# An audio tower whose four engines' instruction sequences are written out in another order

## The reference, cut to what matters

```python
h = gelu(x @ W1 + b1); h = gelu(h @ W2 + b2)            # 750 x 512, exact gelu
lens = sigmoid(h @ W3 + b3); lens = lens / sum(lens) * 375
cs = cumsum(lens); P = max(cs[:, None] - arange(375), 0)
h = warp_weights(P) @ x                                 # 375 x 128
a = layernorm(h); q, k, v = split(rmsnorm(a) @ w_qkv)   # k and v get 8 memory columns
out = rmsnorm((softmax(k) @ v.T  applied to softmax(q)) @ w_out + b_out); h = h + out
xf = layernorm(h); expert = argmax(xf @ switch.T); p = max(softmax(xf @ switch.T))
pos = place of the token among all tokens of its expert so far
h = h + where(pos < capacity, xf @ W[expert].T + b[expert], xf) * p
```

## Time and profile before

| What | us |
|---|---|
| Runs, median (lowest to highest of three) | 393.8 (393.59 to 2108.33) |
| Profiled execution: span from first to last instruction | 392.4 |
| Median less that span | 1.4 |
| PE busy in it | 374.4 |
| DVE busy | 335.1 |
| ACT busy | 227.2 |
| POOL busy | 111.8 |

### The profile page before, as it was taken

One profiled execution on the slowest core, in us unless ns is written; L12 is line 12 of the kernel. 1 busy time (PEld: TensorE's weight loads), 2 busy tenths in 40 slices (PEclk: granted clock), 3 DMA queues, 4 the chain that ended last, 5 costly groups with the idle time before them and its releaser, 6 DMA issues. The chain is left out here.

```text
span 392.4 us, 7891 instructions
## 1 busy us (share of the span) xinstructions
PE 374.4 (95%) x2702; PEld 327.1 (83%) x2702; DVE 335.1 (85%) x916; ACT 227.2 (58%) x433; POOL 111.8 (28%) x136
## 2 busy tenths in 40 slices
PE   8999899999999999999999999999999989999892
PEld 8887788888889888888988888888887788998892
DVE  4687869969897999799988999899998975888896
ACT  4653369627971699159933994389537743782200
POOL 6121301031152216221522141403330501107880
PEclk9999999999999999999999999999999999999998
DMA  7768002002000110002000200100000070331134
GB/s 222 193 197 272 2 1 85 3 0 82 5 20 3 27 62 22 3 0 85 14 10 1 86 7 15 47 0 3 22 0 0 22 195 7 89 118 33 41 80 126
DMA packets 16406, 21.58 MB, mean 55 GB/s; under 512 B 4930, under 2 KB 11928, under 8 KB 15934
## 3 DMA queue, kind: packets, MB, share of 16 engines
q1 hardware_dynamic: 12398, 18.30, 16.1%
q0 software_dynamic: 2880, 2.35, 2.4%
q10 hardware_dynamic: 1088, 0.42, 0.4%
HBM read 14.40 MB, written 6.62 MB: 54 GB/s over the span
## 5 line engine op out<-in xcount | busy, mean ns | idle before, releaser
L1093 PE MATMUL psB<-W2h,h1l 128*125 128x512 f32 x184 | 74.6, 406 | 0.0
L1094 PE MATMUL psB<-W2l,h1h 128*125 128x512 f32 x184 | 72.5, 394 | 0.0
L1095 PE MATMUL psB<-W2h,h1h 128*125 128x512 f32 x184 | 72.5, 394 | 0.0
L668 ACT ACTIVATE h2b<-h2b 125x512 f32<-125x512 f32 x48 | 30.0, 628 | 30.9 <-DVE h2b L1640 30.5
L1095 PEld LDWEIGHTS psB<-W2h,h1h 128*125 128x125 f32 x184 | 34.1, 185 | 8.5
L1094 PEld LDWEIGHTS psB<-W2l,h1h 128*125 128x125 f32 x184 | 34.2, 186 | 6.9
L1093 PEld LDWEIGHTS psB<-W2h,h1l 128*125 128x125 f32 x184 | 34.2, 186 | 6.9
L1640 DVE TENSOR_TENSOR h2b<-psB,b2r 125x512 f32<-125x512 f32 x48 | 32.8, 685 | 4.5 <-PE psB L1095 4.4
L651 ACT ACTIVATE h<-psA,b1c 128x376 f32<-128x376 f32 x60 | 33.3, 579 | 5.7 <-PE psA L1040 3.9
L1647 DVE CUSTOM_DVE_ANT_0 h2b<-h2b,W3r 125x512 f32<-125x512 f32 x48 | 32.9, 690 | 1.6 <-ACT h2b L668 1.4
L531 POOL TENSOR_TENSOR dx<-xt 125x640 f32<-125x640 f32 x8 | 12.9, 1617 | 64.6 <-PE psC L1118 53.0
(11 more groups left out here) (284 smaller groups left out, 970.0 us busy)
## 6 DMA issues: line engine op xcount, KB each, us to landing
xTf<-in_x_t SPq DMA_DIRECT2D x16, 187.5 KB, 2.5
xt<-in_x SPq DMA_DIRECT2D x8, 336.0 KB
slot_x<-eb_parts SPq DMA_DIRECT2D x2, 960.0 KB, 11.9
basef<-in_L_tok_W SPq DMA_DIRECT2D x4, 256.0 KB, 5.3
ewT<-in_expert_t SPq DMA_DIRECT2D x1, 1024.0 KB, 8.0
ewf<-slot_x SPq DMA_DIRECT2D x2, 480.0 KB, 6.2
h2b<-slot_x SPq DMA_DIRECT2D x2, 480.0 KB, 8.2
slot_y<-h SPq DMA_DIRECT2D x4, 240.0 KB, 2.4
```

The lines of the kernel that those rows point to most:

```text
L668: nc.scalar.activation(slot, slot, ACT.Gelu).then_inc(c_g2.sem, 1)
L1093: mm(ps, lo, W2h[:, k, :], start=k == 0, stop=False)
L1094: mm(ps, hi, W2l[:, k, :], start=False, stop=False)
L1095: last = mm(ps, hi, W2h[:, k, :], start=False, stop=k == HK - 1)
```

## The change

`pipeline`, `step`, `opening` and `ending` are gone from TensorE, VectorE, ScalarE and GpSimd, and every call stands in a list, row by row, in another sequence. The calls are the same ones with the same arguments; functions, buffers, waits inside the functions, and SyncE's list stay. ScalarE's `setup` is now called inside `memory_keys` and TensorE's inside `sums`, for row 0 alone. The sequence differs in the opening, in each of the middle rows (which no longer follow one pattern) and in the ending. On ScalarE the exponentials and the gelus of a row stand in fewer separate runs: its list holds 30 table loads before and 19 now. `root_table`, a dummy square root, moves from the middle of the tail to its end.

```diff
 # GpSimd
-            def step(m, f, k, r):
-                if f is not None:
-                    sigmoid_pow(f, before(f))
-                if r is not None:
-                    scatter(r, before(r))
-                if m is not None:
-                    differences(m, before(m))
-                if f is not None:
-                    norm1(f, before(f))
...
-            def opening():
-                differences(0, None)
-                sigmoid_pow(0, None)
-                differences(1, 0)
-                norm1(0, None)
...
+            differences(0, None)
+            sigmoid_pow(0, None)
+            norm1(0, None)
+            differences(1, 0)
+            sigmoid_pow(1, 0)
...
+            counts(0, None)
+            scatter(0, None)
+            differences(2, 1)
+            sigmoid_pow(2, 1)
...
+            counts(3, 2)
+            scatter(3, 2)
+            differences(5, 4)
+            sigmoid_pow(5, 4)
...
+            fetch(3, 0, 3)
+            fetch(4, 0, 3)
+            fetch(0, 0, 3)
+            fetch(1, 0, 1)
+            fetch(1, 1, 3)
+            fetch(2, 0, 3)
+            fetch(5, 0, 3)
 # ScalarE
-                gelu2(LAST, 4)
-                memory_keys(PRIOR, 3)
-                gelu2(LAST, 5)
...
+            memory_keys(6, 1)
+            memory_keys(6, 2)
+            memory_keys(6, 3)
+            route_exp(5, 4)
+            key_exp(6, 5, 0)
+            key_exp(6, 5, 1)
+            key_exp(6, 5, 2)
+            gelu2(7, 2)
+            gelu2(7, 3)
+            gelu2(7, 4)
+            gelu2(7, 5)
 # TensorE
-                expert_products(6)
-                expert_products(7)
-                values(LAST, PRIOR, 1)
-                k_transposed(LAST, PRIOR, 0)
-                k_transposed(LAST, PRIOR, 1)
-                positions(PRIOR, None)
-                k_transposed(LAST, PRIOR, 2)
-                values(LAST, PRIOR, 2)
...
+            values(7, 6, 1)
+            values(7, 6, 2)
+            positions(6, None)
+            expert_products(5)
+            expert_tokens(7)
+            k_transposed(7, 6, 0)
+            k_transposed(7, 6, 1)
+            k_transposed(7, 6, 2)
+            expert_products(6)
+            expert_products(7)
+            chosen_on_rows(6)
+            context(7, 6)
 # VectorE
-                take_outputs(5)
-                query_sum(LAST, PRIOR)
-                take_outputs(7)
-                key_sum(LAST, PRIOR)
-                query_norm(LAST, PRIOR)
-                place_in_expert(PRIOR, PRIOR - 1)
...
+            place_in_expert(6, 5)
+            take_outputs(5)
+            query_sum(7, 6)
+            key_sum(7, 6)
+            query_norm(7, 6)
+            take_outputs(7)
+            own_experts(6)
```

More of the change, by code:

```diff
@@ new lines, in _ @@
+            bias2(1, 0, 5)
+            query_norm(0, None)
+            dot3(1, 0, 4)
+            dot3(1, 0, 5)
+            minus_z(1, 0)
+            scan(1, 0)
+            h1_lower(2, 1, 0)
+            lengths(1, 0)
+            warp_weights(1, 0)
+            bias2(2, 1, 0)
+            take_m(0, None)
+            x_lo_next(2)
+            dot3(2, 1, 0)
+            h1_lower(2, 1, 1)
+            moments1(1, 0)
+            normal1(1, 0)
+            out_norm(0, None)
+            residual(0, None)
@@ new lines, in _ @@
+            place_in_expert(0, None)
+            bias2(2, 1, 4)
+            dot3(2, 1, 3)
+            bias2(2, 1, 5)
+            query_sum(1, 0)
+            key_sum(1, 0)
+            dot3(2, 1, 4)
+            dot3(2, 1, 5)
+            minus_z(2, 1)
+            query_norm(1, 0)
+            scan(2, 1)
+            h1_lower(3, 2, 0)
+            lengths(2, 1)
+            warp_weights(2, 1)
+            bias2(3, 2, 0)
+            probability(0, None)
+            keep_base(0, None)
+            dot3(3, 2, 0)
@@ new lines, in _ @@
+            dot3(4, 3, 3)
+            bias2(4, 3, 5)
+            dot3(4, 3, 4)
+            dot3(4, 3, 5)
+            minus_z(4, 3)
+            query_norm(3, 2)
+            scan(4, 3)
+            h1_lower(5, 4, 0)
+            key_sum(3, 2)
+            probability(2, 1)
+            lengths(4, 3)
+            warp_weights(4, 3)
+            take_m(3, 2)
+            bias2(5, 4, 0)
+            keep_base(2, 1)
+            h1_lower(5, 4, 1)
+            moments1(4, 3)
+            normal1(4, 3)
@@ new lines, in _ @@
+            key_max(4, 3, 2)
+            key_max(4, 3, 3)
+            dot3(5, 4, 1)
+            dot3(5, 4, 2)
+            place_in_expert(3, 2)
+            probability(3, 2)
+            dot3(5, 4, 3)
+            bias2(5, 4, 4)
+            bias2(5, 4, 5)
+            query_sum(4, 3)
+            dot3(5, 4, 4)
+            key_sum(4, 3)
+            dot3(5, 4, 5)
+            minus_z(5, 4)
+            query_norm(4, 3)
+            scan(5, 4)
+            h1_lower(6, 5, 0)
+            lengths(5, 4)
@@ new lines, in _ @@
+            dot3(6, 5, 5)
+            minus_z(6, 5)
+            query_sum(5, 4)
+            scan(6, 5)
+            query_norm(5, 4)
+            lengths(6, 5)
+            warp_weights(6, 5)
+            h1_lower(7, 6, 0)
+            take_m(5, 4)
+            lower_biases()
+            moments1(6, 5)
+            keep_base(4, 3)
+            normal1(6, 5)
+            out_norm(5, 4)
+            residual(5, 4)
+            xn_lo(6, 5)
+            moments2(5, 4)
+            bias2(7, 6, 0)
@@ new lines, in _ @@
+            query_sum(6, 5)
+            dot3(7, 6, 2)
+            dot3(7, 6, 3)
+            keep_h(6, 5)
+            bias2(7, 6, 4)
+            bias2(7, 6, 5)
+            dot3(7, 6, 4)
+            dot3(7, 6, 5)
+            key_max(6, 5, 3)
+            scan(7, 6)
+            query_norm(6, 5)
+            lengths(7, 6)
+            warp_weights(7, 6)
+            keep_base(5, 4)
+            key_sum(6, 5)
+            take_m(6, 5)
+            moments1(7, 6)
+            normal1(7, 6)
+            out_norm(6, 5)
```

1766 lines of the change are left out of this document (1020 added, 746 removed).

## The result

The change made the kernel slower: 409.37 us median (408.98 to 410.1) against 394.22 of the kernel before, a ratio of 1.0393 with a 95% interval of 1.0377 to 1.041. Forecast were 390.5 us and a range of 386 to 395. The profiled execution has a span of 407.3 us, 14.9 more than before.

A forecast was written before the change was run, and what follows sets the result against it. TensorE was taken to bound the kernel up to take_outputs(7), then VectorE with the fetches beside it. -1.0 + 0 + 0.7 - 3.0 = -3.3 on 392.4 gave 389.1, with 1.4 for the median 390.5 us; range 386 to 395.

The forecast's parts named there:

- The middle rows: Five rows of 41 us up to row 7's first layer: no change, at most 1.2 us to gain, new waits up to 3.6.
- Its rule: Rival in two middle rows: scatter and differences delay sigmoid_pow in GpSimd's queue, 1.8 us a row, 3.6 in all; chance 0.12.
- The worst form: GpSimd queue rival at the old distance: sigmoid_pow 4.1 us late in two rows, 1.6 in two more, 401.9 us.
- signs of being wrong: Middle row over 42 us with warp and scan waiting; row 7 to take_outputs(7) under 80; or last stretch still 42.7.
- The opening: Up to row 2's first layer: norm1 put first shortens the wait before xn_transposed(0), -1.0 us, between 0.35 and 1.66.
- Saves 0.35 for certain: Opening: norm1 starts at 45.98 when its input is written, not at 46.33 behind differences(1); the sure part of the gain.
- To `take_outputs(7)`: From row 7's first layer: waits give back 2.3 us, products moved ahead cost 2.97, together +0.7; bounds -0.1 and +2.2.
- To the end: From take_outputs(7): VectorE's chain loses query_norm (1.73) and some of 3.29 us of waits, -3.0; at most 3.8.
- the floor: Fetch chain after take_outputs(7), from the last copy through 18 fetches and finish_row to the output: 38.9 us at least.
- the last two terms: Row 7's first layer to take_outputs(7), +0.7 us, and from there to the end, -3.0 us.
- ScalarE: 0 on the path: 11 fewer table loads free 14.1 us of ScalarE's time, counted as no gain; rival with all gained, 379.7 us, chance 0.03.

The follow-up runs named there:

- e4: The kernel before with GpSimd's list of the changed kernel, fetches kept in the sequence of before: 408.43 us, ratio 1.0358.
- e1: Changed kernel, GpSimd only: differences of rows 2 and 5 back ahead of norm1, scatters of rows 0 and 3 back behind sigmoid_pow: 401.49 us.
- e2: Changed kernel with VectorE's list alone altered in rows 2 to 5: minus_z, query_sum, scan, query_norm in this sequence: 406.28 us.
- e3: Changed kernel with differences and scatters put back at two places on GpSimd, and VectorE's minus_z, query_sum, scan, query_norm in rows 2 to 5: 401.99 us.
- e5: Changed kernel with one layer-1 product repeated on TensorE to fill waits, four times in row 2 and seven in row 5: 407.77 us.
- e9: The kernel before with one exchange on GpSimd: norm1 of row 0 ahead of differences of row 1: 395.91 us, ratio 1.0032.
- e6: Changed kernel with GpSimd's whole list as before, only the fetches in the new sequence: 396.72 us, ratio 1.0079.
- e7: Changed kernel, GpSimd's list as before, VectorE's query_sum ahead of scan and query_norm (rows 2-5), TensorE's sums ahead of q_transposed (rows 2-4): 394.15 us.
- e10: Sequences of e7 up to warp(1), then the kernel before, then the end of e8: 392.17 us, ratio 0.995.
- e8: The kernel before up to the last expert product, then the changed kernel's sequences on all four engines, take_outputs(7) kept behind query_sum(7): 392.64 us.

## Why the prediction was wrong, step by step

**The middle rows: 0, measured +15.9.** This is the step that failed: "the row is full of TensorE work and the new lists keep a layer-1 or layer-2 product at each place where another row is late". TensorE had such products, but too few for 3 us. The prediction saw the place (rows 2 and 5, where scatter and differences stand ahead of `sigmoid_pow`), and took the wrong mechanism for it. Its rule was that the queue decides where index and `minus_z` lie less than 7.66 us apart, with 1.8 us a row. (The 1.8 is a slip, too: 4.1 less the 3 that it puts between the two is 1.1.) In the changed kernel the index is there at 103.3, `minus_z` at 111.07, so by that rule nothing is lost; the rows lost 5.4 and 6.0. The worst form, 4.1 a row, is what e4 measures (3.50), and it is not what the change does. In its place the runs showed these terms. `differences` meets `dot3`: 2.2 and 2.0 us in rows 2 and 5 (e1). `query_norm` meets `sigmoid_pow`: 1.4 us in rows 2, 4 and 5 (e2, e3); in row 3 of the changed kernel `sigmoid_pow` first stands 0.84 behind a scatter and then takes 2.04, so there the queue has a share. `query_sum` ahead of `minus_z` makes that one 1.6 us later (e1 against e3). And the waits that these make let the clock fall: 1.6 and 2.5 us (e5). TensorE's products cover a part of this, so the terms add up to more than the rows lost. Of its signs of being wrong a middle row over 42 us came, and `scan` waiting for `sigmoid_pow` (1.26); `warp` did not wait for `A` there, since TensorE waits earlier, ahead of `q_transposed` and `sums`.

The sign of it stood in the rows. The earlier trace rows has 0.47 us for the last instruction of the moments, and the prediction used it as a duration. In the changed kernel, where `differences` starts later, the same instruction is

```profile
44.93 0.17 DVE L1964 TENSOR_SCALAR rs<-mv 125x3 f32<-125x3 f32 x1
...
46.07 2.21 DVE L1975 TENSOR_SCALAR xn<-h,mv,rs 125x128 f32<-125x128 f32 x3 [0.37 <-POOL rs L531]
```

so 0.30 of the 0.47 were `differences` holding it: the step ends 0.03 us after the first instruction of `differences` (43.87 + 2.08 = 45.95). That one in turn, 2.08 us beside a `dot3`, takes 1.56 in row 2 of the changed kernel, so the 2.46 that the prediction took for `differences` were a stretched figure as well. The Trainium skill, "SBUF — State Buffer", section "Who interferes with whom", says that VectorE and GpSimd share a pair of ports under an exclusive lock: a VectorE step with two inputs in SBUF, or one in a two-port mode, and a GpSimd step that reads SBUF fully block each other, and the one that issues first holds the other. The runs agree on both directions (2.87 against 0.68, 2.80 against 1.33) and on `query_sum`, a reduction, which does not hold `sigmoid_pow`. That rule speaks against this change, and the prediction did not weigh it.

**The opening: -1.0, measured -0.1.** "Saves 0.35 for certain" failed. `normal1` starts 1.16 earlier (46.07 against 47.23) but meets `differences`, takes 2.21 instead of 0.86, and `xn_transposed(0)` starts at 48.34, 0.2 later than in the earlier trace rows, though `warp(0)` had begun 0.4 earlier (39.10 against 39.50):

```profile
48.34 0.54 PE L1272 MATMUL psC<-ident,xn 125*128 125x125 f32 x3 [2.26 <-DVE xn L1975]
```

The -0.1 is that of one execution: in e1, e2 and e3, whose sequences are the same up to there, `warp(0)` begins at 39.65 to 39.95. e9 shows the step alone as a loss. The other sequences did gain in the first rows: row 1 is 1.0 us shorter in e6, e7 and e10, where GpSimd's list is the old one.

**To `take_outputs(7)`: +0.7, measured +1.9.** The cost of the products put ahead of the last expert product was a little small: the stretch of the earlier trace rows with 18.45 us is now 21.86, 3.4 more and not 2.97. The stretch ahead of it gave back 1.5 and not 2.3, and TensorE's idle time in it only fell from 3.76 to 3.19: the 0.78 before the last `keys` went, as forecast, and so did the 0.70 before `warp(7)`, which was to stay, but others came. One of these, 1.09 before an `xf_transposed`, stands behind `normal2(5)`, which takes 2.10 us beside `differences(7)`.

**To the end: -3.0, measured -2.7.** Right in size, with some luck: the 3.0 were taken from VectorE's chain, and what decided was the fetch chain. GpSimd's last fetch and VectorE's last `finish_row`:

```profile
398.83 1.28 POOL L573 DMA_INDIRECT A<-slot_y,idx_g  x1 [0.30 <-issue]
...
403.79 0.88 DVE L2222 SCALAR_TENSOR_TENSOR A<-A,ck,basef 125x128 f32<-125x128 f32 x3 [1.97 <-DMA A<-slot_y,idx_g]
```

That `finish_row` waits, as was forecast, but for a fetch that lands 4.9 us after its issue and not the 3.6 of the earlier trace rows; so the floor was 40.0 us and not 38.9, and 2.7 was all that could go. Most of it was a shift and no gain, as e7 and e8 show: with the products and `query_norm` ahead, e7 ends `take_outputs(7)` 2.1 us later than e8, counted from the start of `warp(7)`, and needs 2.0 less from there to the end. Together the last two terms gave -0.8, where -2.3 were forecast.

**ScalarE: 0 on the path.** Right in the main. Its busy time fell by 13.9 us (14.1 forecast), and no run shows a gain that is its own: e7, which has the changed ScalarE list throughout, is as fast as the kernel before. But the new sequence puts a wait of its own into row 3, where the `gelu1` that TensorE needs stands behind two exponentials and a table load (ScalarE, then TensorE):

```profile
150.49 1.28 ACT L670 ACT_TABLE_LOAD   x1
...
153.02 0.41 PE L1178 MATMUL psA<-xTl,W1h 128*128 128x376 f32 x1 [1.10 <-ACT h L653]
```

No run has ScalarE's list alone, so what it is worth by itself is not shown.

## What to carry to other kernels

Before moving a GpSimd step, write down which VectorE steps will run in its window, and the other way round: a step of one engine can double or quadruple one of the other without any semaphore between them, and the profile shows it only as a longer record of the same shape. So compare the durations of one line and shape across the rows of a trace; the odd one out marks a collision. And price a wait on TensorE with the slower products behind it: here 3 us of wait cost 1.6 and 2.5 more.

## What was not expected of the hardware

Which VectorE steps were held by `differences`: `dot3`, `h1_lower`, `residual`, the lower half of the next input (all with two inputs in SBUF), and `normal1` and `normal2` (one input and scalars). Not held beside it: `bias2` (one input in PSUM), the batch statistics, `key_max`. The small pow steps of GpSimd (125x3) held nothing: in the changed kernel two two-input steps from 133.24 on take their usual 1.00 us together beside one of 1.09 us that began at 132.94, and no step of VectorE beside such a pow, in any of the traces, is more than 0.03 us longer than is usual for it. So the length of a GpSimd record is not the time for which it holds VectorE.

Who was first is not always to be read from the records: `dot3` at 107.06 begins 0.75 us before `differences` at 107.81, beside the last scatter, and still ends 0.56 after its first instruction. Beside a scatter alone `dot3` takes 0.68 (e4). What held it in that 0.75 us stays open.

The same wait ahead of `xn_transposed(0)` did not always end the same way. In the changed kernel (2.26 us) and in e1, e2 and e3 (2.25) the granted clock stayed at 1.00 behind it; in e5 (2.25), e4 and e9 (2.43) it fell. In e9 it differs from one execution to the next: five of the twelve have a mean clock of 0.994 or 0.995 and take 394.3 to 395.4 us (the kernel before 393.6 to 395.2), and seven have 0.990 to 0.992 and take 395.9 to 396.6. So most of e9's loss goes with the clock. What decides whether it falls stays open.
